# Normalising the first image's features inside the first pass, in two tiles that stay allocated

## The reference, cut to what matters

```python
x = conv_general_dilated(sx, w_down, strides (2, 2), feature_group_count=256)   # (8, 256, 64, 64): "downsampled"
xx = x[0].reshape(c, h * w)                                # image 0: 256 channels of 4096 positions
xs = (xx - mn) / jnp.maximum(mx - mn, 1e-12)               # mn, mx: per channel
labels = _kmeans_labels(xs)                                # 10 iterations on 256 points, then a last labelling
v5 = einsum('bchw,ck->bkhw', x, soh / ...)                 # means of every image over the clusters
mu, var = _gmm_fit(...)                                    # 10 iterations
y = sigmoid(...); gate = y[:, slabel]
up = repeat(gate * x + x, 2, axis=1) * w_up
x = bilinear_up_x2(up) + sx                                # layer 0
# layer 1: 64 frequencies of every channel are projected, a small attention is made of them,
# and its output is added to x
```

## Time and profile before

| | us |
|---|---|
| three timed runs: lowest, median, highest | 2626.4, 2627.66, 2629.55 |
| the profiled execution: its time | 2623.3 |
| its span in the trace | 2621.5 |
| TensorE busy in the span | 2318.4 (88%) |
| VectorE busy | 2144.2 (82%) |
| ScalarE busy | 1185.6 (45%) |
| GpSimd busy | 925.9 (35%) |

### The profile page before, as it was taken

One profiled execution on the slowest core, in us unless ns is written; L12 is line 12 of the kernel. 1 busy time (PEld: TensorE's weight loads), 2 busy tenths in 40 slices (PEclk: granted clock), 3 DMA queues, 4 the chain that ended last, 5 costly groups with the idle time before them and its releaser, 6 DMA issues.

```text
span 2621.5 us, 51999 instructions
## 1 busy us (share of the span) xinstructions
PE 2318.4 (88%) x20691; PEld 1566.8 (60%) x20691; DVE 2144.2 (82%) x2312; ACT 1185.6 (45%) x3170; POOL 925.9 (35%) x644
## 2 busy tenths in 40 slices
PE   6999999999995775865998989899999998999887
PEld 2222222222221632434988988888888888888787
DVE  3889989989987425563998999889889998899897
ACT  0101001001000202324777777677777776777774
POOL 1211111112110000001665655556555555555554
PEclk9999999999997896996999999999999999999999
DMA  9999999999994725006999999999999999999998
GB/s 363 388 389 388 389 389 356 378 389 389 389 387 146 303 119 89 0 0 264 361 418 409 417 418 416 418 415 400 417 395 417 418 406 416 413 402 418 412 413 346
DMA packets 493922, 921.78 MB, mean 352 GB/s; under 512 B 211713, under 2 KB 212097, under 8 KB 491266
## 3 DMA queue, kind: packets, MB, share of 16 engines
q1 hardware_dynamic: 284802, 616.61, 61.0%
q0 software_dynamic: 69632, 268.45, 25.2%
q10 hardware_dynamic: 139264, 33.59, 5.8%
HBM read 615.00 MB, written 303.56 MB: 350 GB/s over the span
## 4 chain that ended last, share of the span: by engine, by line
DMA 21%; PE 20%; DVE 5%; ACT 4%; issue 3%; POOL 2%; SPq 0%; POOLq 0%; DVEq 0%; ACTq 0%
PE second_o L1239 14%; DMA second_dd<-downsampled 10%; DMA out<-second_x 8%; DMA second_x<-in_x 2%; PE second_mid_t L1209 2%; DVE second_x L1476 2%; POOL second_left L1024 2%; PE second_st L1099 1%; ACT second_mid L1341 1%; ACT second_left L1353 1%; DVE second_mid L1457 1%; DVE second_left L1024 1%; PE second_zt_t L1222 1%; ACT second_mid_copy L1362 1%; ACT second_part L1341 0%
## 5 line engine op out<-in xcount | busy, mean ns | idle before, releaser
L1239 PE MATMUL second_o<-second_right,second_left 128*128 128x128 f32 x8192 | 1074.9, 280 | 118.2 <-issue 44.4
L1239 PEld LDWEIGHTS second_o<-second_right,second_left 128*128 128x128 f32 x8192 | 991.0, 194 | 153.4 <-issue 143.1
L1024 POOL TENSOR_TENSOR second_left<-second_mid_copy,second_coef_rep 64x1024 f32<-64x1024 f32 x256 | 609.4, 2381 | 941.5 <-ACT second_mid_copy L1362 914.4
L1476 DVE SCALAR_TENSOR_TENSOR second_x<-second_o,second_shift,second_x 128x512 f32<-128x512 f32 x1024 | 727.7, 737 | 132.4 <-PE second_o L1239 119.9
L278 PE MATMUL first_conv<-first_x,first_band 64*64 64x512 f32 (+2 forms) x6144 | 548.6, 616 | 20.0 <-DMA first_x<-in_x 20.0
L252 ACT ACTIVATE first_staged<-first_conv 128x512 f32<-128x512 f32 x128 | 76.6, 598 | 739.7 <-issue 389.3
L278 PEld LDWEIGHTS first_conv<-first_x,first_band 64*64 64x64 f32 (+1 forms) x6144 | 166.4, 118 | 393.4 <-issue 383.4
L217 DVE TENSOR_TENSOR first_product<-first_freq,first_cols 128x4096 f32<-128x4096 f32 x64 | 283.2, 4425 | 124.0 <-PE first_freq L302 121.9
L202 POOL TENSOR_TENSOR first_band<-first_shift,first_w_all 128x576 f32<-128x576 f32 x128 | 145.6, 1159 | 647.2 <-PE first_conv L278 639.9
L1341 ACT ACTIVATE second_mid<-second_dd,all_inter 128x128 f32<-128x128 f32 x1024 | 313.8, 390 | 59.6 <-DMA second_dd<-downsampled 56.9
L1341 ACT ACTIVATE second_part<-second_dd,all_inter 128x128 f32<-128x128 f32 x1024 | 313.7, 390 | 3.2
(11 more groups left out here) (231 smaller groups left out, 1460.8 us busy)
## 6 DMA issues: line engine op xcount, KB each, us to landing
first_x<-in_x SPq DMA_DIRECT2D x128, 2048.0 KB, 21.5
second_x<-in_x SPq DMA_DIRECT2D x256, 1024.0 KB, 19.3
out<-second_x POOLq DMA_DIRECT2D x256, 1024.0 KB, 10.8
downsampled<-first_staged ACTq DMA_DIRECT2D x512, 64.0 KB, 10.9
second_dd<-downsampled SPq DMA_DIRECT2D x64, 512.0 KB, 20.5
gather_two<-downsampled SPq DMA_DIRECT2D x4, 2048.0 KB, 14.7
gather_four<-downsampled SPq DMA_DIRECT2D x4, 2048.0 KB, 19.1
gather_raw<-downsampled SPq DMA_DIRECT2D x3, 2048.0 KB, 10.4
```

The source lines that it names most:

```text
L1024: return eng.tensor_tensor(left[a][rows, odd:HALF:2, :, :].rearrange("p n (t s) g -> p n t s g", t=T), turned[rows, :, :, :].unsqueeze(3). ...
L1239: last = nc.tensor.matmul(ob[n][:, r, :], left[a][:, r, n, :], right[a][:, r, :], start=True, stop=True)
L1476: nc.vector.scalar_tensor_tensor(out=xt[i][:, n // S, n % S, rows, :], in0=ob[n][:, :, :], scalar=shift[:, n:n + 1], in1=xt[i][:, n // S, ...
```

## The change

Two tiles of 16 KB a partition, `image[0]` and `image[1]`, are allocated around the whole program. In the first pass `image[1]` serves as the seventh input slot, and the other six slots are as before. `image[0]` is an additional tile: at group 40 SP's queue loads `xd[0, 0]` into it, and VectorE normalises it in place in three steps, behind its work for groups 43 (maximum), 47 (minimum) and 51 (the rest). After the last group and the last store SP loads `xd[0, 1]` into `image[1]`, ahead of the writes of the sums. The gather pass takes `image` as `xx0` and `xx1`; VectorE normalises only half 1, in place, at once; TensorE transposes half 0 as soon as the constants are there. The constants are loaded first, and the seven slabs of the first batch, which include the raw halves of image 0 for the means, are issued behind them without a wait. In the second pass `image` gives the first two of the four input buffers.

```diff
-def first_pass(nc, x, w_rows, first_cols, xd, xp, xpd):
+def first_pass(nc, x, w_rows, first_cols, xd, xp, xpd, image):
...
-        xt = [sc.sb(f"x{i}", [P, B, BLOCK1, W]) for i in range(SLOTS1)]
+        xt = [sc.sb(f"x{i}", [P, B, BLOCK1, W])[:, :, :, :] for i in range(SLOTS1 - 1)]
+        xt.append(image[1].rearrange("p (b r w) -> p b r w", b=B, r=BLOCK1))
+        hi, lo, den, inv = (sc.sb(n, [P, 1]) for n in ("hi", "lo", "den", "inv"))
...
                     if g == GROUPS1 // 2:
                         store_freq(0, GROUPS1 // 2)
+                    if g == IMAGE_LOAD:
+                        for i in range(STAGED):
+                            sp.wait_ge(stored[i], len(range(i, pairs // 2, STAGED)) * 64)
+                        sp.dma_start(image[0], xd[0, 0, :, :]).then_inc(image_in[0], 16)
+
+                sp.wait_ge(freq_made, GROUPS1)
+                for i in range(STAGED):
+                    sp.wait_ge(stored[i], len(range(i, pairs, STAGED)) * 64)
+                sp.dma_start(image[1], xd[0, 1, :, :]).then_inc(image_in[1], 16)
                 store_freq(GROUPS1 // 2, GROUPS1)
                 sp.wait_ge(low_summed, GROUPS1 // SPAN)
                 sp.dma_start(xpd, low_freq[:, :, :, :].rearrange("p n b v -> p n (b v)")).then_inc(low_out, 16)
-                for i in range(STAGED):
-                    sp.wait_ge(stored[i], len(range(i, pairs, STAGED)) * 64)
+                sp.wait_ge(image_in[1], 16)
...
+                def normalise(step):
+                    if step == 0:
+                        dve.wait_ge(image_in[0], 16)
+                        ch.link(nc.vector.tensor_reduce(hi[:, :], image[0], AX.X, ALU.max))
+                    elif step == 1:
+                        ch.link(nc.vector.tensor_reduce(lo[:, :], image[0], AX.X, ALU.min))
+                    else:
+                        ch.link(nc.vector.tensor_tensor(den[:, :], hi[:, :], lo[:, :], ALU.subtract))
+                        ch.link(nc.vector.tensor_scalar(den[:, :], den[:, :], 1e-12, None, ALU.max))
+                        ch.link(nc.vector.reciprocal(inv[:, :], den[:, :]))
+                        ch.link(nc.vector.tensor_scalar(image[0], image[0], lo[:, 0:1], inv[:, 0:1],
+                                                        ALU.subtract, ALU.mult))
...
                     sum_cols(g)
+                    if g in NORMALISE:
+                        normalise(NORMALISE.index(g))
...
+IMAGE_LOAD = 40
+NORMALISE = (43, 47, 51)
...
+        slab["xx0"], slab["xx1"] = image
...
-                for t in range(T):
-                    load(0, t)
                 sp.dma_start(cst[:, :], consts).then_inc(const_in, 16)
-                for t in range(T):
-                    sp.wait_ge(d_in[0][t], 16)
-                for b, t in ((2, 0), (4, 0), (6, 0), (2, 1), (4, 1)):
+                for b, t in ((0, 0), (2, 0), (4, 0), (6, 0), (0, 1), (2, 1), (4, 1)):
                     load(b, t)
...
-                for t in range(T):
-                    col = slice(t, t + 1)
-                    dve.wait_ge(d_in[0][t], 16)
-                    nc.vector.tensor_reduce(hi[:, col], raw[t], AX.X, ALU.max)
...
+                col = slice(1, 2)
+                nc.vector.tensor_reduce(hi[:, col], xx[1], AX.X, ALU.max)
...
-                    if n == 0:
-                        pe.wait_ge(normal, t + 1)
+                    if n == 0 and t == 1:
+                        pe.wait_ge(normal, 1)
...
-        xt = [sc.sb(f"x{i}", [P, T, S, ROWS2, W]) for i in range(XBUF)]
+        xt = [image[i].rearrange("p (t s h w) -> p t s h w", t=T, s=S, h=ROWS2) for i in range(T)]
+        xt += [sc.sb(f"x{i}", [P, T, S, ROWS2, W])[:, :, :, :, :] for i in range(T, XBUF)]
```

More of the change, by code:

```diff
@@ L136, in first_pass @@
         const_in, cols_in = sc.sem("const_in"), sc.sem("cols_in")
+        image_in, norm_chain = [sc.sem(f"image_in{t}") for t in range(T)], sc.sem("norm_chain")
         x_in = [sc.sem(f"x_in{i}") for i in range(SLOTS1)]
@@ L235, in sum_low_cols @@
                     nc.vector.tensor_reduce(low_freq[:, n, :, :], room, AX.X, ALU.add).then_inc(low_summed, 1)
+                ch = Chain(dve, norm_chain)
+                def normalise(step):
[10 more added lines that the diff above has]
+                                                        ALU.subtract, ALU.mult))
                 for g in range(GROUPS1):
@@ L335, with gather_pass @@
 WIDE = P // K
-def gather_pass(nc, cst, consts, xd, ohn, oh_t, ft, work, pieces):
+def gather_pass(nc, cst, consts, xd, ohn, oh_t, ft, image, work, pieces):
     with Scope(nc, "gather") as sc:
-        slab = {n: sc.sb(n, [P, POS])[:, :] for n in ("raw0", "raw1", "xx0", "xx1", "two0", "two1", "four0", "four1")}
+        slab = {n: sc.sb(n, [P, POS])[:, :] for n in ("raw0", "raw1", "two0", "two1", "four0", "four1")}
+        slab["xx0"], slab["xx1"] = image
         turned = sc.sb("turned", [P, NT, T, P])
@@ L368, in gather_pass @@
         xx = [slab["xx0"], slab["xx1"]]
-        raw = [slab["raw0"], slab["raw1"]]
         with nc.Block() as block:
@@ L405, in _ @@
                 ch = Chain(dve, chain_sem)
[L407 to L416 removed]
+                col = slice(1, 2)
+                nc.vector.tensor_reduce(hi[:, col], xx[1], AX.X, ALU.max)
+                ch.link(nc.vector.tensor_reduce(lo[:, col], xx[1], AX.X, ALU.min))
+                ch.link(nc.vector.tensor_tensor(den[:, col], hi[:, col], lo[:, col], ALU.subtract))
+                ch.link(nc.vector.tensor_scalar(den[:, col], den[:, col], 1e-12, None, ALU.max))
+                ch.link(nc.vector.reciprocal(inv[:, col], den[:, col]))
+                nc.vector.tensor_scalar(xx[1], xx[1], lo[:, col], inv[:, col],
+                                        ALU.subtract, ALU.mult).then_inc(normal, 1)
                 ch.link(nc.vector.memset(placed[:, :, :], 0.0))
@@ L943, with second_pass @@
 Y_LEAD = 16
-def second_pass(nc, x, cst, p_cols, att_cols, inter, wqk_sb, wv_sb, vx, gam, xd, xps, coef, out):
+def second_pass(nc, x, cst, p_cols, att_cols, inter, wqk_sb, wv_sb, vx, gam, xd, xps, coef, image, out):
     xv = x.rearrange("b (t g s) h w -> b t g s (h w)", t=T, s=S)
@@ new lines, in program @@
+    with Scope(nc, "image") as si:
+        image = [si.sb(f"half{t}", [P, POS])[:, :] for t in range(T)]
+        first_pass(nc, x, w_rows, first_cols, xd, xp, xpd.rearrange("(n c) u r -> (c u) n r", n=GROUPS1 // SPAN), image)
+        with Scope(nc, "all") as sc:
+            cst = sc.sb("const", [P, CONST_N])
+            xps = sc.sb("xps", [P, B * T, S, UV])
+            coef = sc.sb("coef", [P, B, T, S])
+            inter = sc.sb("inter", [P, W + 4 * HD])
+            wqk_sb, wv_sb = sc.sb("wqk", [P, TS, P]), sc.sb("wv", [P, TS, C])
+            vx = sc.sb("vx", [UV + 1, C])
+            gam = sc.sb("gam", [P, 1])
+            by_group = xp.rearrange("(t g) a r (c v) -> t a c g r v", t=T, v=LOW)
+            later = [(xps[:, b * T + t, :, :].rearrange("g s (u v) -> g (s u) v", v=LOW),
+                      by_group[t, b // HALF_B, b % HALF_B]) for b in range(B) for t in range(T)]
+            later += [(inter[:, :], inter_cols), (wqk_sb[:, :, :], wqk), (wv_sb[:, :, :], wv),
+                     (vx[UV:UV + 1, :], bias),
+                     (gam[:, :], gamma.rearrange("(a b) -> a b", b=1).broadcast_to([P, 1]))]
+            with Scope(nc, "gates") as sg:
+                ohn = sg.sb("ohn", [P, T, K])
+                oh_t = sg.sb("oh_t", [P, T, P])
+                xpu = sg.sb("xpu", [P, B * T, UV])
+                ft = sg.sb("ft", [P, NT, P])
+                low_group = xpd.rearrange("(t g) u (b v) -> t b g u v", t=T, b=B)
+                later += [(xpu[:, b * T + t, :].rearrange("g (u v) -> g u v", v=LOW), low_group[t, b])
+                          for b in range(B) for t in range(T)]
+                gather_pass(nc, cst, consts, xd, ohn, oh_t, ft, image, wv_sb, xps)
+                feat = sg.sb("feat", [P, NT, P])
+                mixture_pass(nc, cst, w_conv, w_up, ft, feat, oh_t, xps, xpu, coef, later)
+            second_pass(nc, x, cst, p_cols, att_cols, inter, wqk_sb, wv_sb, vx, gam, xd, xps, coef, image, out)
```

31 lines of the change are left out of this document (removed).

## The result

The changed kernel took 2608.66 us in the median of 4 runs (2607.23 to 2611.06), the kernel before beside it 2627.03 (4 runs, 2623.84 to 2629.55). The ratio is 0.9932, 95% interval 0.9914 to 0.9949: 0.68% faster, 18.4 us in the medians. I had forecast 12.5 us and 2615.2 us, with a range from 2610.0; the time is 1.3 us under it. The profiled execution took 2607.23 us (span 2605.5, for 2621.5 before: 16.0 us shorter).

A forecast was written before the change was run, and what follows sets the result against it. TensorE was taken to pace the first pass, with DMA nearly as full, and a dependent chain the gather pass; −15.2 + 2.7 = −12.5 us on the 2627.7 us median gave 2615.2 us, own range 2612.5 to 2618, wider range 2610 to 2621.

The forecast's parts named there:

- applied to the median: Final sum: the 12.5 us gain was taken off the timed median of before, 2627.7 us, giving 2615.2 us.
- step 7: Second pass: its buffers at other places, same count and load order, cost nothing, with 1 us either way.
- TensorE's start: Gather pass: TensorE waits only for the constants, landing 4.4 us after issue; gain 15.2 us, between 11.9 and 17.8.
- Half 1's normalisation: Gather pass: half 1 ready at 853.2, TensorE needs it at 858.8; cover 5.6 us, cost nothing.
- The slabs for the means: Gather pass: seven slabs in the first batch, over 40 us of cover before the means read them; cost nothing.
- The load at the end: First pass's end: half 1's load lands at 829.9, covered by 10.4 us of VectorE's last work; cost nothing.
- VectorE's steps: First pass: three normalising steps behind groups 43, 47, 51 each fit an idle hole of VectorE (4.88 us); cost nothing.
- The load at group 40: First pass: 5.2 us slab less 2.5 us slack stalls group 44 by 2.7 us (2.4 to 3.7), without a clock fall.
- no stall: Rival, first pass: group 44 does not wait, only the gain is left; 2612.5 us, down to 2610; chance 0.12.
- the gain doesn't come through: Rival, gather pass: constants land late, at 854.1, sharing engines with the slabs; gain 4.3 us, 2623.4 us; chance 0.07.
- the deficit doesn't heal: Fourth rival, first pass: DMA queue stays full, groups 44 to 63 all wait; 11.5 us slower, 2639 us; chance 0.05.
- The dearer first pass: Rival: clock falls in the stall (restart 2.5 us) or a second tile is late; 2617.7 to 2620.2 us; chance 0.18.

The follow-up runs named there:

- e1: Kernel before with only the tiles' places those of the changed kernel; loads, waits and normalisation as before: 2621.6 us, ratio 0.9989 to the kernel before.
- e9: Second run of the kernel before with only the tiles' places changed: 2621.28 us, ratio 0.9985 to the kernel before.
- e4: The changed kernel again, unaltered, for a second trace: 2609.51 us, ratio 0.9953 to the kernel before.
- e10: The changed kernel a third time, unaltered, beside the places-only kernel on one chip: 2611.09 us, ratio 0.9952 to the kernel before.
- e2: Changed kernel without the load at group 40 and the three steps; both halves loaded at the first pass's end, normalised in the gather pass: 2615.38 us, ratio 0.9974.
- e8: Changed kernel with the middle load at group 34 and VectorE's steps behind groups 39, 43, 47: 2609.34 us, ratio 0.9942 to the kernel before.
- e3: Changed kernel with the middle load at group 48 and VectorE's steps behind groups 51, 55, 59: 2610.58 us, ratio 0.9947 to the kernel before.
- e6: Changed kernel with the second projection behind the group's own projection instead of ahead of it: 2609.92 us, ratio 0.9951 to the kernel before.
- e11: Changed kernel with the second projection behind the group's own and the middle load at group 48, second run: 2609.46 us, ratio 0.9941 to the kernel before.
- e12: Kernel before with the image tiles allocated behind the first pass, so only later parts have the new places: 2624.14 us, ratio 1.0000.
- e13: Kernel before with a 16 KB a partition tile allocated ahead of the first pass, moving that pass's tiles alone: 2624.34 us, ratio 0.9998.

## Why the prediction missed, step by step

**The priced terms were about right in sum; the base they were applied to was not, and neither was a term put at nothing.** By the six and three traces the change is +3.5 us in the first pass, −16.7 us in gather and mixture, −2.0 us in the second pass (1440.0 to 1443.4 in the old kernels, so no more than scatter but for the first trace after): −13.2 us for the two parts that it touches, where my sum was −12.5; 1.5 us too little of gain and 0.8 us too little of stall cancel in part. The two repeated comparisons have ratios of 0.9953 and 0.9952, 12.3 and 12.6 us, and medians 15.1 and 14.4 us apart. The first had 18.4 us, from four runs each, and its interval (13.4 to 22.6 us) leaves the 12.5 out.

The first step that failed is "applied to the median": 2627.66 was the median of three runs, and 72 later runs of before have medians of 2624.6 to 2625.4. The second is step 7, the places at nothing "with 1 us either way": e1 and e9, with only the places changed, are 3.0 and 4.2 us under before in the medians. The 6.5 us by which 2615.2 was too high split in two ways, as two comparisons have before, the kernel with only the places changed, and the changed kernel on one chip. All figures are from medians, and one of five runs is itself uncertain by a microsecond or two.

| us by which the forecast was too high | before, e1, e4 | before, e9, e10 |
|---|---|---|
| the base, 2627.66, over before's median there | 3.0 | 2.2 |
| the places, put at nothing | 3.0 | 4.2 |
| the schedule, 12.1 and 10.2 us for my 12.5 | −0.4 | −2.3 |
| the repeat (2609.51, 2611.09) over the first four runs (2608.66) | 0.9 | 2.4 |

The last row is luck of the sample. That the miss lay on the fast side, although the first pass was dearer than I had summed, is due to the base, to the sample, and to places whose effect nothing here explains.

1. *TensorE's start.* Right in kind; the size is 16.7 and not 15.2 us. TensorE started 3.9 us after the constants' issue (850.82 − 846.92; 3.9 in e4 too), not 4.5. The Trainium skill's page DMA: Bandwidth & Descriptors ("Anatomy of one DMA") has a fit for DMAs issued by GpSimd, by which their landing would be at 3.4 us as an estimate, for my 4.4; these loads are SP's, and the row lies between the two. Another 0.6 us is TensorE's own: from its start to the first k-means round 31.0 us for 31.6, its first 32 transposes taking 5.31 us for 5.90. The granted clock stood at 0.50 in both when it started and rose earlier, about 3.3 us behind the start for about 4.5 us before, as the stretches after show (last three columns: granted clock, DMA share, GB/s):

```profile
851.00:853.00 2.00, 2.00 (x10) 2.00 (x11) 2.00 (x2) 0.77 (x2) 0.00 (x0) 0.50 1.08 459
853.00:855.00 2.00, 2.00 (x16) 2.00 (x15) 2.00 (x1) 1.60 (x4) 0.00 (x0) 0.71 1.03 434
855.00:857.00 2.00, 2.00 (x21) 2.00 (x20) 1.86 (x5) 2.00 (x6) 0.00 (x0) 1.00 0.93 393
```

2. *Half 1's normalisation* free: right; ready at 858.7, taken at 863.1, cover 4.4 us. e2 shows the price without the early half, 8.7 us more in gather and mixture.
3. *The slabs for the means* free: right. The means' first matmul is at 945.27, right behind k-means, for 956.17.
4. *The load at the end* free: right: from the last write of the sums to the gather pass's first load there are 4.4 us (842.47 to 846.92), no more than the 4.9 us of before.
5. *VectorE's steps* free: right.
6. *The load at group 40*: the stall by slack is right (2.5 and 3.1 us for 2.7; 1.2 us where TensorE was late already; 3.65 for 3.4 in e8). What failed is "nor should the clock fall in it". I had read from the end of the first pass that the upper level lasts at least 3.8 us of standing, and taken a shorter wait to be safe. In e4 the level did last through the wait, and fell when TensorE was at work again (the stretches above); that a fall can come behind a wait which is over is what the step left out. The clock fell behind waits of 1.96, 2.54, 2.83, 3.10 and 3.65 us (e3 at group 60, e4, e6, e10, e8), in e8 alone before TensorE had resumed. It stayed up behind all other waits of the first pass from its second group on, of which the longest are 1.82 us (after) and 1.96 us (e11): at 1.96 us there is one of each. So the slab at group 40 costs 2.5 + 1.6 = 4.1 us in e4, 4.7 in e10, 4.4 in e6, and 1.2 in the first trace after; the mean over the three traces of the changed kernel is 3.3 us, close to the 3.5 us that the first pass lost. The three traces differ in their waits for ScalarE's copies too, so that the two means agree this well is partly luck. e2's first pass ends at 841.5, so without the added load nothing is lost.
7. *Places* at nothing, within 1 us: two comparisons say 3 to 4 us for all places together, by their intervals 0.5 to 5.2 and 1.6 to 6.3 us. So no effect at all is ruled out by both, and an effect of 1 us by the second. The cause is open: e12 and e13, each with a part of the places, say nothing, and no part of the traces of e1 and e9 is shorter by as much. The schedule alone then gives 12.1 us (e4 against e1) or 10.2 us (e10 against e9).

Of the rivals, "no stall", "the gain doesn't come through" and "the deficit doesn't heal" are refuted by the rows above. The dearer first pass is what happened in two of the three traces of the changed kernel; I had put the restart at 2.5 us, and it costs 1.6. Its time did not come out at 2617.7 or more for the reasons above. Against the fourth rival I had read an issue of 0.37 us as the sign of a drained queue; it was the shortest of four whose longest was 5.87 us, and in the changed kernel an issue of 0.43 us stands right between two of 5.47 and 11.30 us. That row did not show what I took from it, though the deficit did heal.

## What to carry to other kernels

Where a load is put into a full queue, its price is the bytes' time less the slack of the tile behind it, and the same slab makes TensorE wait 0.8 to 2.0, 1.2 to 3.1 or 3.7 us by where it is put (groups 48, 40, 34); behind most of the longer of these waits the restart costs 1.6 us more, so a place that shortens the wait a little can save twice. A saving of 15 us ahead of a dependent chain comes through whole. Here a sum made on one trace came within 1 us of the traces' difference in the parts that it priced; a median of three runs as its base cost 2 to 3 us, and a term put at nothing without a row for it 3 to 4 us. To tell 3 us in 2625 took 11 runs and more of each kernel.

## What the runs showed of the hardware

The clock that TensorE is granted did not fall by the length of the standstill alone. It was still up 3.8 us behind the last matmul of the first pass. In e4 it was at 1.00 through a standstill of 2.54 us and at 0.50 from 1.6 us after its end. Behind a standstill of 1.96 us it fell in e3 and stayed up in e11. From a row of one standstill no safe length can be read, nor from the clock's level while the engine stands.

The engine that issues a DMA into a full queue is held by it, and its next instruction with it. The timeline of the changed kernel at group 28: ScalarE's issues of four 64 KB stores take 5.2 to 5.9 us (1.83 us at the end of the pass, with the queues empty), so its copy comes late, and TensorE's second projection behind it.

```profile
372.45 5.91 ACTq L287 DMA_DIRECT2D downsampled<-first_staged  x4
378.48 0.60 ACT L281 ACTIVATE first_staged<-first_conv 128x512 f32<-128x512 f32 x1 [6.06 <-PE first_conv L307]
379.11 5.19 ACTq L287 DMA_DIRECT2D downsampled<-first_staged  x4
379.13 1.92 PE L345 MATMUL first_low_freq_ps<-first_staged,first_low_rows 128*32 128x512 f32 x16 [1.66 <-ACT first_staged L281]
```

Two copies and eight stores are 2 x 0.60 + 5.91 + 5.19 = 12.3 us, and with the small gaps between them the same copy comes again after 12.59 us (371.83 and 384.42). TensorE needs 12.07 us for a plain group and 12.49 us on the mean of four, of which one takes 13.75. So in this stretch ScalarE, held by its own stores, falls behind by 0.1 us a group, and nothing in the busy shares (45%) says so. The kernel before has the same spacing there (356.27 and 368.86) and no wait; what decides between the two is not shown. And SP's issue of the 2 MB slab took 5.47 us, the 2 MB tile behind it 0.43 us and the next one 11.30 us: the length of an issue says when there was room in the queue, not how large the load is.
